# Third pass of a two-layer kernel: for one channel of eight, the slope-weighted rectified values are added by DVE instead of by a second matmul

## The reference, cut to what matters

```python
h = sign(batchnorm1(gn(x1)))          # +1 / -1
h = grouped_conv3x3(h, sign(w)) * sw  # scale per output channel
h = batchnorm2(h) + gn(x1)
out = x1 + where(h > 0, h, a * h)     # a: one slope per channel
```

## Time and profile before

| | |
|---|---|
| profiled execution, its own time | 4701.64 us |
| its span | 4699.4 us |
| median of three runs | 4704.78 us |
| PE busy over the span | 4509.8 us, 96% |
| DVE busy | 4235.9 us, 90% |
| ACT busy | 3861.5 us, 82% |
| GpSimd busy | 1478.8 us, 31% |
| data moved | 1612.17 MB, mean 343 GB/s |
| granted TensorE clock, mean | 0.992 |

### The profile page before, as it was taken

The page is one execution under the profiler, slowest core; times in us unless marked ns, Lnnn a source line. Parts: engine busy times, 40 slices in busy tenths (PEclk is TensorE's granted clock), DMA queues, the critical chain, the costliest instruction groups (busy, mean ns, idle before and its releaser), DMA issues.

```text
span 4699.4 us, 83432 instructions
## 1 busy us (share of the span) xinstructions
PE 4509.8 (96%) x21948; PEld 2748.6 (58%) x22204; DVE 4235.9 (90%) x10523; ACT 3861.5 (82%) x5517; POOL 1478.8 (31%) x3481
## 2 busy tenths in 40 slices
PE   6999999999999979999999996999999999999999
PEld 6999999999999974433333332444444444444444
DVE  6999999999999989999999997888888888888887
ACT  7999999999999967777777774777777777777776
POOL 4888888888888880000000000000000000000000
PEclk9999999999999999999999998999999999999999
DMA  5888888888888879999999996999999999999998
GB/s 202 318 317 316 318 319 318 317 318 320 321 317 317 317 282 351 370 369 368 368 368 368 369 368 252 377 375 376 374 376 375 376 377 374 377 375 375 376 376 297
DMA packets 686229, 1612.17 MB, mean 343 GB/s; under 512 B 30002, under 2 KB 423986, under 8 KB 620658
## 3 DMA queue, kind: packets, MB, share of 16 engines
q1 hardware_dynamic: 686194, 1611.76, 95.0%
HBM read 940.55 MB, written 671.10 MB: 343 GB/s over the span
## 4 chain that ended last, share of the span: by engine, by line
PE 76%; POOL 6%; ACT 6%; issue 5%; DVE 5%; DMA 1%; SPq 0%; DVEq 0%; POOLq 0%; ACTq 0%
PE psV L1007 13%; PE psT L1066 12%; PE psV L1066 12%; PE psT L1082 8%; PE psT L1084 7%; PE psV L1084 7%; PE psV L1082 7%; PE psT L990 7%; DVE ring_x L952 4%; ACT ring_y L675 3%; PE psV L1004 3%; POOL ring_y L481 2%; ACT ring_g L584 1%; POOL u_r L495 1%; POOL x_r L457 1%
## 5 line engine op out<-in xcount | busy, mean ns | idle before, releaser
L1007 PE MATMUL psV<-W0T,ring_gT 128*128 128x128 f32 x8192 | 1080.0, 275 | 47.6 <-issue 34.0
L1007 PEld LDWEIGHTS psV<-W0T,ring_gT 128*128 128x128 f32 x8192 | 1076.8, 192 | 33.6
L770 DVE BATCH_NORM_STATS2 early<-ring_z 128x6 f32<-128x128 f32 x4096 | 822.7, 274 | 0.0
L761 DVE SCALAR_TENSOR_TENSOR ring_z<-psV,x_r,ring_x 128x1024 f32<-128x1024 f32 x512 | 657.2, 1284 | 117.3 <-DVE early L770 76.9
L665 ACT ACTIVATE late<-ring_x,minus_b 128x512 f32<-128x512 f32 x1024 | 639.5, 707 | 1.3 <-PE psV L1084 1.3
L632 ACT ACTIVATE ring_x<-ring_x,bn_c 128x1024 f16<-128x1024 f32 x512 | 604.2, 1229 | 31.0 <-DMA bn_c<-bn_scratch 31.0
L850 DVE BATCH_NORM_STATS2 h_tup<-ring_x 128x6 f32<-128x512 int16 x1024 | 619.4, 668 | 0.0
L481 POOL TENSOR_SCALAR ring_y<-ring_z,u_r,u_nm 128x1024 f32<-128x1024 f32 x512 | 605.8, 1199 | 35.6 <-POOL gn L500 35.6
L964 DVE SCALAR_TENSOR_TENSOR ring_x<-ring_x,bn_q,psV 128x512 f32<-128x512 f32 x512 | 376.1, 744 | 255.2 <-PE psV L1084 254.9
L590 ACT ACTIVATE ring_g<-ring_x,x_ms 128x1024 f32<-128x1024 f32 x512 | 585.3, 1143 | 0.0
L675 ACT ACTIVATE ring_y<-ring_y,gnb 128x512 f32<-128x512 f32 x512 | 368.0, 801 | 239.7 <-DVE ring_x L952 202.3
(11 more groups left out here) (150 smaller groups left out, 5857.6 us busy)
## 6 DMA issues: line engine op xcount, KB each, us to landing
ring_x<-in_x SPq DMA_DIRECT2D x128, 2048.0 KB, 8.8
y_scratch<-ring_y SPq DMA_DIRECT2D x128, 2048.0 KB, 12.7
ring_x<-y_scratch SPq DMA_DIRECT2D x512, 512.0 KB, 6.2
out<-ring_x SPq DMA_DIRECT2D x256, 1024.0 KB, 14.0
h_scratch<-ring_x SPq DMA_DIRECT2D x256, 512.0 KB, 6.1
ring_y<-y_scratch SPq DMA_DIRECT2D x128, 1024.0 KB, 7.3
ring_z<-y_scratch SPq DMA_DIRECT2D x128, 1024.0 KB, 7.4
ring_g<-h_scratch SPq DMA_DIRECT2D x64, 1024.0 KB, 11.6
```

The lines of the kernel that those rows point to most:

```text
L761: dve.scalar_tensor_tensor(out=ring_z[:, c % 2, cols], in0=psV[:, j % 2, :], scalar=x_r[:, s, j:j + 1], in1=ring_x[:, s, cols], op0=ALU.mu ...
L770: last = dve.bn_stats(z_tup[:, s, j, 2 * r:2 * r + 2, :].rearrange("p h t -> p (h t)"), ring_z[:, c % 2, SL * j + 2 * S * r:SL * j + 2 * S ...
L1007: last = pe.matmul(psV[:, j % 2, P * r:P * (r + 1)], ring_gT[:, j, P * r:P * (r + 1)], W0T[:, :], start=False, stop=(r % 4 == 3))
```

## The change

One constant names the channel m of a tile, 7 of 0 to 7, that is handled in the new way. DVE gets one more instruction per tile at the start of `finish`: t_slot[7] = relu_slot(7) * (1 - a) + t_slot[7], in place, with a semaphore `fused`. It waits for the relu of m = 7 of that tile. PE issues for m = 7 only the identity matmul (start and stop both true) and does not wait for the relu. ACT's relu of m = 7 waits for `fused` of the tile before, where it waited for `combined`. DVE's `finish` of m = 7 waits for `fused` as well as `combined`.

```diff
+ON_DVE = 7
...
+        fused = sem("fused")
...
                     if from_round(i, c, 1):
-                        act.wait_ge(combined, 8 * t + m - 7)
+                        if m == ON_DVE:
+                            act.wait_ge(fused, t)
+                        else:
+                            act.wait_ge(combined, 8 * t + m - 7)
...
                 t = SLOTS * i + c
+                own = 8 * (c % 2) + ON_DVE
+                dve.wait_ge(relu_done, 8 * t + ON_DVE + 1)
+                dve.scalar_tensor_tensor(out=t_slot(c % 2)[:, ON_DVE], in0=relu_slot(ON_DVE), scalar=one_less[:, own:own + 1],
+                                         in1=t_slot(c % 2)[:, ON_DVE], op0=ALU.mult, op1=ALU.add).then_inc(fused, 1)
                 if from_round(i, c, 2):
                     dve.wait_ge(out_stored[c % 2], 32 * (2 * i + c // 2))
                 for m in range(8):
                     ch = 8 * (c % 2) + m
+                    if m == ON_DVE:
+                        dve.wait_ge(fused, t + 1)
                     dve.wait_ge(combined, 8 * t + m + 1)
...
                 for m in range(8):
-                    pe.wait_ge(relu_done, 8 * t + m + 1)
                     if from_round(i, c, 1):
                         pe.wait_ge(added, 8 * t + m - 7)
+                    if m == ON_DVE:
+                        pe.matmul(sum_bank(m), ident[:, :], y3_slot(s)[:, :, m, :],
+                                  start=True, stop=True).then_inc(combined, 1)
+                        continue
+                    pe.wait_ge(relu_done, 8 * t + m + 1)
```

## The result

| | before | after |
|---|---|---|
| median of four runs each | 4704.05 us | 4647.85 us |
| profiled span | 4699.4 us | 4643.6 us |
| ratio, with its 95% interval | | 0.9881 [0.9866, 0.9896] |

The change makes the kernel 56.2 us faster. It is the time of the rival that was named "compute sets the pace", 4651 us, to within 3 us; the range ended at 4652 us, just above what that rival had forecast.

What follows compares the result with a forecast made beforehand. PE and the DMA engines were both taken as full in pass 3, with DMA limiting after the change: 127 x (13.957 - 13.85) = 13.6 us plus 4 us once, 17 to 18 us faster, giving 4688 us, range 4652 to 4714.

Steps and rivals of the forecast that it cites:

- compute sets the pace: Rival: compute engines pace pass 3 and DMA speeds up with demand; 4651 us, partly so up to 4675; chance 0.22.
- The DMA floor of 13.85 us a tile: Pass 3 transfers: with engines at share 1.01, a tile could shrink only 0.11 us, from 13.957 to 13.85 us.
- the dips in it "will stay": Recurring drops of the DMA share, as at 4018 us, would remain; that one is 0.16 of 0.31 us shortfall.
- the 4 us "once" before DMA would hold the pass: Pass 3: about 4 us gained once at compute pace, until `finish` waits for the output stores.
- The loop and the PE tile: Pass 3: PE tile's end to next but one's start, 14.1 us, averaged with PE tile 12.97: 13.53 us, 54 us gain.
- DVE's instruction: New DVE instruction before `finish`: 0.66 us a tile, covered by DVE's 1.97 us of waiting for PE.
- The waits added: New waits of DVE, ACT and `finish` around m = 7 are already satisfied when reached and cost nothing each.
- No change: Rival: DMA has nothing left, floor 13.92 us or more, PE just idles; 4696 to 4714 us; chance 0.22.
- slower: Rival: longer queue makes loads meet the previous tile's stores, 14.15 us a tile; 4729 us (4715 to 4735); chance 0.16.
- the cases built on the share: Main case, pass 3: DMA holds at a somewhat shorter tile, 4676 to 4695 us; chance 0.40.
- the marks set out to tell the cases apart: Trace signs: 378 to 380 GB/s and stores landing after 17 to 19 us if right; 385 GB/s or more if compute paces.

Runs made afterwards that it cites:

- DMA alone: Kernel whose pass 3 moves the same bytes with the same issues but leaves out nearly all computing; 4480.1 us, 12.49 us a tile.
- the kernel with one matmul more: Kernel before the change with one more float32 matmul per tile, overwritten by the next one; 4784.3 us, ratio 1.0175.
- the kernel with halves and one channel on DVE: Changed kernel with `affine` in two image halves, each with its own signal to ACT; 4562.2 us, ratio 0.9700.
- the run with DVE's half alone: Changed kernel with PE's second matmul of m = 7 put back, so that term is added twice; 4702.7 us, ratio 1.0000.
- the one with PE's half alone: Kernel before the change without the second matmul of m = 7, nothing in its place; 4646.3 us, ratio 0.9883.
- the kernels with three and with four channels on GpSimd: Second matmul of three or four channels replaced by two GpSimd instructions each, without DVE's new instruction; 5008.4 us and 5131.8 us.
- the kernel with two channels on DVE: Changed kernel with channels m = 6 and 7 handled on DVE instead of only 7; 4593.0 us, ratio 0.9771.

## Why the prediction was wrong

**The DMA floor of 13.85 us a tile.** This is the step that failed, and it alone gives the miss. From a share of 1.01 the prediction concluded that at most 0.31 us and probably 0.11 us a tile could be won, and that the dips in it "will stay". DMA alone needs 12.49 us. The rows that it read already held windows with a share over 1, up to 1.08, so a share of 1 was no ceiling. The dips went away as the pace rose, beside full computing too. Of 240 windows of 1 us (3600 to 3680, 4000 to 4080 and 4200 to 4280), 42 had a share under 0.9 in the kernel with one matmul more, 22 before, 12 after, 5 in the kernel with halves and one channel on DVE, and none with DMA alone. That kernel with halves ran at 407 GB/s beside full computing, so any floor beside the computing lies at its own pace of 12.9 us or below; where between 12.49 and 12.9 was not measured. The sum took the higher of two limits on the time of a tile, as it should, and the false one was the higher. With it fell the 4 us "once" before DMA would hold the pass: no row has DVE waiting for the output DMA.

**The compute side was right.** The loop and the PE tile, (14.1 + 12.97) / 2 = 13.53 us, and 54 us of gain: 13.54 us and 56.2 us were measured. The loop's turns alternate between 14.18 and 14.00 us before, a mean of 14.09, which gives (14.09 + 13.83) / 2 = 13.96 before and (14.09 + 12.98) / 2 = 13.53 after. That the prediction shortened its one reading of 14.18 to 14.1 was in part luck: one of the spans that it averaged ends at 4035.34, where PE starts without having waited for the loop.

**DVE's instruction.** 0.66 us, hidden under its waiting: shown by the run with DVE's half alone and the one with PE's half alone. The waits added cost nothing that the trace shows.

**No change, and slower.** Both rested on the same false floor; no run shows the pace of DMA brought down by a longer queue or by loads that meet stores. With DMA alone the stores landed after 17.0 us in place of 14.1, and the throughput was the highest of all runs.

**The chances.** The row that spoke for the right rival stood in the prediction: no compute engine waits for a DMA in 1200 us. That rival was given 0.22, and the cases built on the share 0.40, with 0.22 more for no change. That no engine waits for a DMA is direct evidence that DMA does not pace; a share of busy time is no evidence that it does. Of the marks set out to tell the cases apart, two came out for the rival: 387 GB/s where 385 or more was to mean that compute paces, and stores that land after 14.8 us where 17 to 19 was forecast.

## What to carry to other kernels

A busy share of 1.0 on the DMA engines does not show that they are at their limit; look for a compute engine that waits for a landing, and where there is none, measure the floor with a kernel that moves the bytes and leaves out the computing. In this kernel, where an engine's work on one tile is followed by a chain over other engines back to its work on the next but one, the tile takes the mean of the two as long as the chain is longer: work taken from the engine gives back half, and so does a shorter chain, until they meet. Cut the chain first, then the whole saving counts: signal a half-finished result so that the next engine can start.

## What the runs showed of the hardware that was not expected

- With DMA alone the DMA engines moved 420 GB/s in a mix of three parts loads in 8 KB pieces and two parts stores in 2 KB pieces; the time recorded as busy for the bytes of a tile varied from 12.9 us at that pace to 14.3 us in the kernel with one matmul more.
- A GpSimd tensor-tensor instruction beside DVE's `affine` made this two to three times as long, 1.08 to 1.48 us in place of 0.48, or was itself held up, 3.00 us in place of 1.04. The two kinds of GpSimd instruction took 1.44 and 1.31 us on average.
- TensorE's granted clock fell where PE waited long. Windows of the kernels with three and with four channels on GpSimd, in which PE was busy for 76% and 66% of the stretch, then two short ones of the first kernel and a matmul in each:

```profile
3300.00:4400.00 1100.00, 836.59 (x1744) 358.09 (x1743) 978.59 (x1669) 717.70 (x1077) 547.14 (x403) 0.86 0.88 319
```
```profile
3300.00:4400.00 1100.00, 725.63 (x1506) 310.37 (x1504) 965.22 (x1579) 667.32 (x1002) 678.57 (x504) 0.82 0.83 300
```
```profile
3990.00:3992.00 2.00, 2.00 (x3) 0.67 (x2) 2.00 (x6) 2.00 (x5) 0.00 (x0) 0.50 0.93 328
...
3996.00:4000.00 4.00, 4.00 (x11) 1.77 (x10) 2.06 (x3) 4.00 (x7) 3.92 (x4) 1.00 0.99 315
```
```profile
3991.35 1.91 PE L1109 MATMUL psT<-late,early 128*128 128x512 f32 x2
...
3996.51 1.02 PE L1109 MATMUL psT<-late,early 128*128 128x512 f32 x2
```

The means of 0.86 and 0.82 are made of two levels. PE had waited 7.99 us for ACT before 3989.48; just after it the clock stood at 0.50, the lower level of 1.2 GHz, and from one matmul to the next it was 1.70 us (3991.35 to 3993.05). From 3996 on it stood at 1.00, the level of 2.4 GHz, and a matmul took 0.86 us. In the kernel with two channels on DVE, where PE waited for 1.0 us at most, the clock was 1.00 over 1100 us, and with DMA alone, where PE had no work, 0.50. Part of the loss of the GpSimd kernels is this; how much was not measured.
